# Other lags and another order of VectorE's stages in the last layer's pass over the edges

## The reference

```python
q = x[dst] @ Wq_w + Wq_bias
key_base = x_src @ Wk1 + rel_emb @ Wk2 + Wk_bias
scores = (score_base[:, None] + score_rule) * scale
attn = vmap(seg_softmax)(scores, dst)          # softmax over the edges of one target
mean_attn = attn.mean(axis=1)
msg = x_src @ W_r[edge_type]
out = segment_sum(msg * mean_attn[:, None], dst) + bias
out = relu(layernorm(out) * ln_g + ln_b)
```

## Time and profile before

| | us |
|---|---|
| median of 3 runs | 8520.82 (8500.45 to 8528.5) |
| the profiled execution's own time | 8492.32 |
| its span, first to last instruction | 8490.5 |
| PE, PEld busy | 5200.4, 3779.8 |
| DVE, ACT, POOL busy | 4832.2, 4211.9, 4967.0 |

### The profile page before, as it was taken

How to read it: one execution, slowest core, us unless ns; L and a number is a source line. 1 busy time by engine, 2 the same in 40 slices (tenths; PEclk the granted TensorE clock), 3 DMA queues, 4 the chain that set the end, 5 groups by cost and what they waited for, 6 DMA issues and landing times. The chain is left out here.

```text
span 8490.5 us, 161453 instructions
## 1 busy us (share of the span) xinstructions
PE 5200.4 (61%) x38193; PEld 3779.8 (45%) x38194; DVE 4832.2 (57%) x21267; ACT 4211.9 (50%) x11643; POOL 4967.0 (59%) x5713
## 2 busy tenths in 40 slices
PE   4666666666664444444444448997666666666664
PEld 3555555555552222222222226885444444444443
DVE  5555555554545555555555568996555555555556
ACT  3445555554523434343433348994554555555554
POOL 5555555555535555555555547994555666565663
PEclk8888888887876666666666668998676666676666
DMA  4233333333334444444444446885222222222221
GB/s 116 83 87 87 87 87 87 88 86 86 87 90 128 128 129 128 126 129 129 128 128 126 128 120 218 267 268 205 59 62 60 63 63 63 61 63 62 63 63 42
DMA packets 672779, 908.53 MB, mean 107 GB/s; under 512 B 141174, under 2 KB 429928, under 8 KB 672441
## 3 DMA queue, kind: packets, MB, share of 16 engines
q1 hardware_dynamic: 502366, 605.50, 23.0%
q0 software_dynamic: 168944, 301.30, 14.6%
q10 hardware_dynamic: 1357, 0.47, 0.0%
HBM read 696.57 MB, written 210.28 MB: 107 GB/s over the span
## 5 line engine op out<-in xcount | busy, mean ns | idle before, releaser
L785 POOL DMA_INDIRECT rows<-src_rows,idx_slots x1563 | 1499.0, 959 | 1172.3 <-DVE pre L1504 600.5
L785 POOL DMA_INDIRECT rows<-rel_rows,idx_slots x1563 | 1499.3, 959 | 1022.5 <-issue 409.8
L785 POOL DMA_INDIRECT rows<-node_rows,idx_slots x1371 | 1310.2, 956 | 999.4 <-issue 366.7
L1391 ACT ACTIVATE onehot<-ident,fresh_slots 128x128 f32<-128x128 f32 x3136 | 992.9, 387 | 899.2 <-remote 643.4
L1382 PE MATMUL bank<-onehot,ones 128*128 128x512 f32 x1568 | 1304.1, 928 | 4.3 <-ACT onehot L1391 4.3
L1480 PE MATMUL bank<-w_e,edge_in 128*128 128x256 f32 x784 | 427.3, 645 | 1402.7 <-DVE onehots L867 945.4
L1089 ACT ACTIVATE dst_pairs<-pre,minus_node 128x512 bf16<-128x512 int16 x816 | 577.6, 719 | 1145.7 <-remote 757.9
L1480 PEld LDWEIGHTS bank<-w_e,edge_in 128*128 128x128 f32 x784 | 189.6, 293 | 1855.0 <-issue 938.0
L1119 PE MATMUL bank<-by_chunk,dst_pairs 128*128 128x192 bf16 x6144 | 791.3, 275 | 260.8 <-issue 145.4
L1119 PE MATMUL bank<-wide_room,dst_pairs 128*128 128x192 bf16 x3264 | 488.8, 283 | 548.7 <-ACT dst_pairs L1093 472.4
L1191 DVE TENSOR_SCALAR dst_pairs<-pre,node_at 128x512 bf16<-128x512 int16 x1536 | 545.9, 355 | 467.2 <-remote 309.2
(11 more groups left out here) (307 smaller groups left out, 12151.2 us busy)
## 6 DMA issues: line engine op xcount, KB each, us to landing
edge_in<-dst_line SPq DMA_DIRECT2D x392, 256.0 KB
spill<-rows SPq DMA_DIRECT2D x392, 256.0 KB
rows<-spill SPq DMA_DIRECT2D x392, 256.0 KB, 3.2
hot_rows<-rows SPq DMA_DIRECT2D x98, 712.0 KB
onehots<-hot_rows SPq DMA_DIRECT2D x196, 356.0 KB, 3.5
onehots<-src_low SPq DMA_DIRECT2D x98, 512.0 KB
edge_in<-in_ea_l SPq DMA_DIRECT2D x98, 256.0 KB
edge_in<-in_eaT_l SPq DMA_DIRECT2D x392, 64.0 KB
```

Source lines behind the costliest of these rows:

```text
L785: pool.indirect_dma_start(out=to[:, b.slot(ROW_RING), g, :], out_offset=None, in_=table, in_offset=bass.IndirectOffsetOnAxis(ap=idx_slots[ ...
L1391: last = act.activation(diag[:, b.slot(2), g, :], ident[:, :], ACT.Copy, scale=fresh_slots[:, b.slot(2 * RING), g:g + 1])
```

## The change

The lists of three engines get new lags, and DVE's a new order. `hot` and `look` keep theirs. No stage is added, dropped or rewritten, and no ring changes its size.

```diff
-                        pipeline(act, [(2, far_stage(act, far3, 2, s_hot, s_far, s_spread)),
-                                       (3, shrinks),
-                                       (2, spread_stage(act, s_score, s_diag, s_spread)),
-                                       (4, exps), (4, weigh)])
+                        pipeline(act, [(4, far_stage(act, far3, 2, s_hot, s_far, s_spread)),
+                                       (5, shrinks),
+                                       (4, spread_stage(act, s_score, s_diag, s_spread)),
+                                       (7, exps), (7, weigh)])
...
-                        pipeline(pe, [(1, look), (5, sum_up), (3, find), (2, spread)])
+                        pipeline(pe, [(1, look), (8, sum_up), (5, find), (4, spread)])
...
-                        pipeline(dve, [(3, maxima), (3, running),
-                                       (3, high), (3, left), (0, hot), (3, middle), (3, low),
-                                       (1, scores), (3, take), (3, differ), (5, add), (0, build),
-                                       (3, clamp)])
+                        pipeline(dve, [(5, maxima), (6, take), (5, running), (6, differ), (5, high),
+                                       (6, clamp), (5, left), (0, hot), (5, middle), (8, add),
+                                       (5, low), (3, scores), (2, build)])
```

## The result

| | before | after |
|---|---|---|
| median us (lowest to highest, runs) | 8524.66 (8500.45 to 8534.72, 4) | 8585.28 (8582.19 to 8611.35, 4) |
| profiled execution's own time | 8492.32 | 8585.2 |
| pass of the last layer, first `hot` to last `add` | 2470.3 | 2535.0 |
| one batch in the steady part | 6.32 | 6.50 |

The change makes the kernel slower: the ratio of the runs is 1.0086, 95% interval [1.0066, 1.0105], and the medians are 61 us apart. The direction was forecast, the size was not: 8700 is 175 us above before's median. Between the two profiled executions the pass grew by 65 us. The profiled execution of after also entered the pass 28 us later than that of before, after code that is the same in both; that lies within the spread of the runs and is no part of the effect.

The account below looks back on a forecast made before the run. It took the last layer's pass as bound by turns between engines, none full. POOL's runs add 184 us and the drain 12, 8492 + 196 = 8688; half of the median's 28 us excess makes 8700, range 8350 to 8870.

Parts of the forecast that it names:

- step 1: `scores` on DVE, from 1 to 3 behind `hot`: its 0.66 us a batch of waiting goes, -258 us of idle time.
- step 2: `take`, `differ`, `clamp` interleaved on DVE: `take`'s 0.60 us a batch goes, `maxima` to end of `low` grows from 2.17 to 2.6.
- step 3: Ring of `low`, `find`, `spread`, `maxima` at the lower clock: 5.05 us becomes 5.2, bounds 4.9 and 5.6.
- step 4: `add` ahead of `low` puts all PE work in one ring: 5.54 us at 1.2 GHz, 3.8 at 2.4.
- rival A: Faster: lost DVE waits decide, PE's clock stays high, ring 3.8 us under POOL's 5.0; 8434 or 8277 us, chance 0.33.
- step 5: ACT's order and row slots cost 0; three more drain steps at the pass's end add 12 us.
- How this sets POOL's runs: POOL's gathers: 60% of batches in single runs of 7.23 us, else 6.14, giving 6.79 a batch.
- my own formula: POOL's time a batch: 6.14 + 0.6 x 1.09 = 6.79 us, from 60% single runs.
- the forecast's 184: POOL's longer time a batch over the last layer's pass: +0.47 x 391 = +184 us.
- B: Much slower: every sum late, every batch its own run of 7.23 us, if `add` waits over 1 us; 8860 us, chance 0.19.
- 12 + 14 us: Additions to the forecast time: 12 us for the drain, and half of the runs' median excess of 28 us.
- C: Nothing: `maxima` and `add` take up what `scores` and `take` lose; 8492 + 12 to 8535 us, chance 0.10.

Follow-up runs that it names:

- e5: The changed kernel, unaltered, run again on another chip where updates were on time: 6732.25 us, ratio 1.0013 to before.
- e1: The changed kernel with `add` moved from ahead of `low` to behind `scores`: 6773.93 us, ratio 1.0064 to before.
- e13: The changed kernel with the end of `sum_up` handed on late by SP through a small DMA: 7576.67 us, ratio 1.1275 to before.
- e14: The changed kernel with `add` behind `scores` and `sum_up`'s end handed on late by SP through a small DMA: 6775.0 us, ratio 1.0082 to before.
- e10: Before's lags with the changed kernel's DVE order, `take`, `differ`, `clamp` one batch later and `add` ahead of `low`: 6727.04 us, ratio 1.0001 to before.
- e2: The kernel before with `add` alone moved, from behind `differ` to ahead of `low`, lags kept: 6760.43 us, ratio 1.0043 to before.
- e9: The changed kernel's lags with before's DVE order, `add` behind `low`: 6734.35 us, ratio 1.0015 to before.
- e16: Before's lags with the changed kernel's DVE order, but `add` behind `scores`: 6754.29 us, ratio 1.0032 to before.
- e7: The kernel of e1 run again, beside e5: 6766.08 us, ratio 1.0068 to before.
- e12: The kernel before with the end of `sum_up` handed on late by SP through a small DMA: 6738.94 us, ratio 1.0027 to before.

## Why the forecast had the sign and not the size

1. `scores` (step 1): as forecast. 258 us of waiting became 9, and none of it came off the time.
2. `take` and the longer chain (step 2): `take`'s 236 us went to 0.4. `maxima` to the end of `low` was priced at 2.6 us and bounded below at 2.37; with `add` in it and no wait it is 2.36 (e5), the bound itself. The small operations of the other batch fit the pauses whole.
3. The ring of `low`, `find`, `spread`, `maxima` (step 3): priced 5.2. From the end of `low` to the next `maxima` it is 7248.31 - 7245.60 = 2.71 where before had 2.88, so 0.17 of the 0.28 for `diag` went; 2.36 + 2.71 = 5.07. It does not bind.
4. `add` ahead of `low` (step 4): the waits came where it put them. `add` idles 604.8 / 392 = 1.54 us a batch, and PE waits for it no more. The price of the ring was too low, 5.54 us at the lower clock where it measures 7245.74 - 7239.13 = 6.61 (`find` to `find`). `find` to `look` is 2.21 as priced and `sum_up` 1.37, shorter than priced; the term that failed is the sum's update, put at 0.31 us, which is 1.88 in this turn and 1.5 in the median of the pass. The prediction had itself read late updates from the earlier trace rows, yet took this one as on time. Nor was the ring 3.8 us for a third of the time: half of all its turns take between 6.43 and 6.50 us, since the update waits for POOL's stop whatever PE's clock is. The granted clock of the stage fell, from 0.68 to 0.62; by the two levels that is 76% of the time at 1.2 GHz instead of 64%. The Trainium skill, page "TensorE: Matmul & The Clock Gate", section "Why this matters for your kernels", has continuous work bring the clock up. PE's work is no more continuous than it was: its two waits of 1.25 and 0.63 us a batch became one of 2.03 ahead of `find`. So the trace neither bears the rule out nor speaks against it; it shows that rival A's stream without a pause did not come about.
5. The drain (step 5) was put at +12 us. From the last gather to the last `add` it is 8424.90 - 8389.86 = 35.0 us before and 8517.74 - 8483.21 = 34.5 after: nothing. The steps added are as short as 2.57 us, since little is left in them.

**The step that failed is "How this sets POOL's runs": its term for a run of one batch, 3 x 1.25 + 3.48 = 7.23 us, is 6.52.** I took the 3.48 from the stop of the earlier trace rows that came after eight gathers, and used it for a stop after four. There POOL goes on 7245.78 - 7243.01 = 2.77 us after its last gather began. Before's own trace had that price, 6.47 us in the median of 104 such runs, and the 1.73 us of idle time in the first row was a sign of it. The share of such batches was also off, 60% forecast and 350 of 391, or 90%, measured: the ring never got shorter than POOL's run. With my own formula: 6.14 + 0.6 x (6.52 - 6.14) = 6.37, which takes 165 us off the forecast's 184; the true share puts 0.3 x 0.38 x 391 = 45 us back. 184 - 165 + 45 = 64, and the pass grew by 65. That the two errors have opposite signs is luck: with the share right and 7.23 kept, the miss would have been nearly as large as B's 275 us. The other 12 + 14 us that were added, for the drain and to meet the median, did not come, and the later entry of 28 us, which nothing forecast, made up for them.

Of the rivals, A is out: its sides did lose their waits, yet the clock that it needed did not come. B had the right picture, every sum late and nearly every batch a run of its own, and its condition (`add` waiting over 1 us) is met; the same 7.23 made it 275 us too dear. C is out by the interval.

**What stays open.** What a run of one batch costs, and that nearly all are such runs, is read from the traces. That it is `add`'s place that makes them so, and not the greater lags, is argued from after's trace and from a lateness made by hand. It is not shown by running e1's order where PE's own updates are late: that happened on none of the five chips. What makes the updates late is not known either. And that the record's before could gain by e1's order is not tested; with updates on time it loses 0.5 to 0.7%.

## What to carry to other kernels

An instruction that waits is a gate for all behind it on its engine: where what it waits for is late, put it behind those that feed the next turn of its own chain (e13 against e14, 12.8% against 0.8%). Where it was on time, neither place was the better one in every list: ahead cost nothing in e10 and 0.4% in e2, behind 0.1% in e9 and 0.3 to 0.7% in e16, e1 and e7. Price a ring with the lateness that its updates show in the same trace, and with the engine's pauses as they follow runs of the length you forecast, not the length you happened to look at; count all runs by length before taking one for typical. A change that trades slack for filled pauses can be free where updates are on time and dear where they are not, so it is worth a deliberate delay in one semaphore to see which waits have slack.

## What the runs showed of the hardware

- The same kernel took 8525 us in the record and 6718 to 6733 on the five chips of the studies. The pass holds 2470 - 1961 = 509 us of these 1800; the rest is in the other layers.
- In the record PE's updates of semaphores are late, and more so the longer POOL has issued gathers without a stop. Counting updates more than 0.4 us behind the modelled end of their matmul, by the number of gathers begun since POOL's last stop: in before 19 of 157 after one, 36 of 198 after two, 90 of 221 after three, 169 of 284 after four; in after none of 398, 28 of 310, 229 of 317 and 349 of 352. They come through with a stop: 634 of before's 718 late ones and 496 of after's 636 fall into one, in the median 1.6 and 1.05 us after its last gather. In the studies the same count finds none between their first 32 gathers and the last, though POOL there issues hundreds on end. So gathers alone do not do it. The Trainium skill, page "Perfetto Trace Analysis", section "Tensor Engine Instruction", says that the update comes once PSUM has acknowledged the write. In the studies it comes 0.014 us behind the modelled end. The page gives no time for it, so that the late ones of the record neither agree with it nor speak against it.
- A 32-byte DMA on SP between an engine's update and the one that waits for it made the update about 2 us later (medians of 2.04, 1.95 and 2.07 us in e12, e13 and e14).
